# Scatter DMAs of routed rows placed between GpSimd's multiplications in the state-space scan

## The chip, the cores and the metric

One core of one Trainium2 chip runs the whole program. The metric is the device time of one execution in microseconds. Five engines take part: TensorE (PE in the rows), VectorE (DVE), ScalarE (ACT), GpSimd (POOL) and SyncE (SP), each with its own instruction queue; they meet only through semaphores and DMA completions.

## What is computed

A decoder layer on 32 sequences of 128 tokens with 128 channels: a selective state-space scan (16 states per channel, 256 inner channels), then attention against a context (16 heads of 8), then a mixture of 8 experts of which each token takes two; each of the three is added to its input and normed. Cut to what matters:

```python
xr = x @ W_in;  xs, res = split(xr);  u = silu(causal_conv(xs))
delta = softplus(...);  Bm, Cm = ...                    # from u @ W_x
hs = scan(exp(delta * A), delta * Bm * u)               # 16 states n
y  = einsum('bldn,bln->bld', hs, Cm) + u * D
x  = layernorm(x + (y * silu(res)) @ W_out)
x  = layernorm(x + attention(x, ctx))
x  = layernorm(x + sum_e wte[:, e] * ((silu(x @ w1[e].T) * (x @ w3[e].T)) @ w2[e].T))   # top 2 of 8 experts
```

## The kernel before

The tokens are cut into G = 8 groups of S = 4 sequences, T = 512 tokens each. A loop over m = 0..7 is written out on every engine, in an order set by hand; what follows a wait on an engine stands behind it. Each turn has two parts.

**Scan of group m**: states n = 0..15. For each state GpSimd forms `delta*u*B` (`times_b`, L420, into a ring of three buffers, so the product for state n + 3 waits for state n's scan), ScalarE forms the decay (`decay`, L588), VectorE runs two `tensor_tensor_scan` (`states`, L861) and, but for four states, multiplies by C (`times_c`, L868). States 2, 6, 9 and 12 (`POOLED`) are multiplied by C on GpSimd instead (`times_c`, L427, into one buffer `hc_pool`). TensorE adds each product into `y_ps` (`y_add`, L1339), broadcasts the B and C rows (L1315, L1326), and in between does convolutions and projections for groups m + 1 and m + 2. On TensorE the order around the last pooled product is fixed: row C 14, `y_add` of state 12, `y_add` of 13, residual, row C 15, `y_add` of 14, `y_last` (L1344). On GpSimd it is: `times_b` for 12 (at n = 9, behind `times_c` 9), 13, 14, 15 (at n = 10, 11, 12), then `times_c` for 12.

**Stage after the scan** (called the tail below, until attention's first exponentials): TensorE's output projection `first_out` (L1379), `values` (L1368), 12 matmuls that only keep it busy (L1387), transposes (L1396), queries (L1402), scores (L1424); VectorE's statistics (L899), norm (L914) and rotary products; ScalarE's exponentials (L623). GpSimd meanwhile makes the masks (`masks`, L440 and L443), scatters rows, adds a bias (`add_bo`, L454, which waits for VectorE's norm) and forms the next group's step sizes (L404, L406).

**The scatter**: once the top-2 experts of a group are known, each row of x2 goes to two places of the table `xg` in HBM. For group w that is eight indirect DMAs (4 sequences x 2 experts, 128 rows of 520 bytes each), L461, all on GpSimd's queue. Their places `pos` are written by VectorE at state n = 1 of scan w + 2 (`spots_out`). The experts' stage, which reads `xg`, begins after the last group. The scatters of groups 6 and 7 stand behind the loop.

SyncE issues loads in order: context and mask of the next group (the mask's after `masks`), then x three groups on, after `first_out`.

Of the kernel before, what the change touches and what calls it, by code (L numbers as in the profile page):

```python
# [14 lines left out]
S = 4  # L15
# [24 lines left out]
def build(nc, a, out):  # L40
    ctx = ExitStack()
    with ctx:
        def sb(name, shape, dt=F32):
            return ctx.enter_context(nc.sbuf_tensor(name, shape, dt))

        def sem(name):
            return ctx.enter_context(nc.semaphore(name))
# [99 lines left out]
        x2_all = sb("x2_all", [P, B, ROW])  # L147
# [10 lines left out]
        pos = sb("pos", [P, S, 2], I32)  # L158
# [51 lines left out]
        xg = nc.dram_tensor("xg", (E * STRIDE + P, ROW), F32, kind="Internal").ap()  # L210
# [13 lines left out]
        s = {n: sem(n) for n in names}  # L224
# [39 lines left out]
        def pooled_done(m, n):  # L264

            return len(POOLED) * m + POOLED.index(n) + 1
# [8 lines left out]
        def at(eng, name, count):  # L275
            if count > 0:
                eng.wait_ge(s[name], count)

        def parts(m):

            return (m - 1 if m else None), (m + 1 if m + 1 < G else None), (m + 2 if m + 2 < G else None)
# [84 lines left out]
        def _(pool):  # L366
# [34 lines left out]
            def step_size(m):  # L401
                at(pool, "softp", m + 1)
                at(pool, "a_ps", 2 * NST * m)
                g_.tensor_tensor(delta[:, :, :], zpos[:, :, :], zabs[:, :, :], ALU.add).then_inc(s["delta_sb"], 1)  # L404
                at(pool, "delta_sb", m + 1)
                g_.tensor_tensor(du[:, :, :], delta[:, :, :], u[:, m % 2], ALU.mult).then_inc(s["du_sb"], 1)  # L406
                at(pool, "du_sb", m + 1)
                for h in range(2):
                    last = g_.memset(delta[:, h, :].rearrange("p (s t) -> p s t", s=S)[:, :, 0:1], RESET)
                last.then_inc(s["delta_set"], 1)  # L410

            def times_b(m, n):
                at(pool, "du_sb", m + 1)
                at(pool, "b_sb", NST * m + n + 1)
                if n < 3:
                    at(pool, "s_ps", 16 * m)
                    at(pool, "h_sb", 2 * NST * m)
                else:
                    at(pool, "h_sb", 2 * (NST * m + n - 3) + 2)
                g_.tensor_tensor(bu[:, n % 3], du[:, :, :], b_row[:, n % 3, :].unsqueeze(1).broadcast_to((P, 2, T)), ALU.mult).then_inc(s["bu_sb"], 1)  # L420

            def times_c(m, n):
                at(pool, "h_sb", 2 * (NST * m + n) + 2)
                at(pool, "c_row_sb", pooled_done(m, n))
                before = POOLED.index(n) - 1
                at(pool, "y_sum", 17 * m + (POOLED[before] + 1 if before >= 0 else 0))
                g_.tensor_tensor(hc_pool[:, :, :], hst[:, n % 3], c_row[:, :].unsqueeze(1).broadcast_to((P, 2, T)), ALU.mult).then_inc(s["hc_pool_sb"], 1)  # L427

            def b_low(m, n):
                at(pool, "bc_mid_s", m + 1)  # L430
                if m:
                    at(pool, "hc_pool_sb", pooled_done(m - 1, 6))
                at(pool, "bu_sb", NST * (m - 1) + n)
                at(pool, "scat", (m - 3) * 2 * S * 16)
                g_.tensor_tensor(bc3[64:96, m % 2, :], bc_rest[64:96, :], bc_mid[64:96, :], ALU.subtract).then_inc(s["bc3_low"], 1)
                at(pool, "bc3_low", m + 1)

            def masks(g):
                at(pool, "mask_load", 16 * g + 16)
                g_.tensor_scalar(pad[:, :], mask_b[:, :], 0.0, NEG, ALU.is_equal, ALU.mult).then_inc(s["pad_sb"], 1)  # L440
                at(pool, "pad_sb", g + 1)
                at(pool, "s_ps", 16 * g)
                g_.tensor_tensor(mbias[:, :, :], pad[:, :].rearrange("p (s t) -> p s t", s=S),  # L443
                                 causal[:, :].unsqueeze(1).broadcast_to((P, S, L)), ALU.add).then_inc(s["mask_sb"], 1)

            def add_k(g):
                at(pool, "rotk_sb", 2 * g + 2)
                at(pool, "k_heads_sb", 4 * g)
                g_.tensor_tensor(qk[:, 1, :], rotk[:, 0, :], rotk[:, 1, :], ALU.add).then_inc(s["k_sb"], 1)

            def add_bo(g):
                at(pool, "x1_sb", S * g + S)
                at(pool, "wo_ps", 2 * g)
                g_.tensor_tensor(x1b[:, :, :], x1[:, :, :], bo_b[:, :].unsqueeze(1).broadcast_to((P, S, D)), ALU.add).then_inc(s["x1b_sb"], 1)  # L454

            def scatter(w):
                at(pool, "pos_sb", w + 1)
                at(pool, "row_sb", w + 1)
                for t in range(S):
                    for k in range(2):  # L460
                        pool.indirect_dma_start(xg[:, :], bass.IndirectOffsetOnAxis(ap=pos[:, t, k:k + 1], axis=0),  # L461
                                                x2_all[:, w * S + t, :], None).then_inc(s["scat"], 16)

            b_low(0, 0)
            for n in range(3):
# [1 line left out]
            for m in range(G):  # L467
                w, e, c = parts(m)
                for n in range(NST):
                    if n in POOLED and n != 12:  # L470
                        times_c(m, n)
                    if n + 3 < NST:
                        times_b(m, n + 3)
                    if n == 12:
                        times_c(m, n)
                    if n == 6 and e is not None:
                        b_low(e, 10)
                if m == 0:
                    at(pool, "w_later", 16 * NL)
                    add_k(0)  # L480
                masks(m)
                if m >= 2:
                    scatter(m - 2)
                add_bo(m)
                if e is not None:
                    at(pool, "q_sb", 2 * m + 1)
                    step_size(e)
                    add_k(e)
                    for n in range(3):
                        times_b(e, n)  # L490
            scatter(G - 2)
            scatter(G - 1)

            with pool.Fori(0, NT // 8) as it:
# [1209 lines left out]
```

## Time and profile before

| | |
|---|---|
| median of 3 runs | 1159.5 us (1154.22 to 1162.19) |
| the profiled execution | 1163.2 us |
| its span, first to last instruction | 1161.4 us |
| PE busy | 1022.0 us (88%) |
| DVE busy | 804.3 us (69%) |
| ACT busy | 759.5 us (65%) |
| POOL busy | 600.3 us (52%), with 64 scatter DMAs in 62.5 us |
| mean granted TensorE clock | 0.962 |

Busy shares are means over stages with different limits: GpSimd's 52% is made of stretches in which it has no gap and of long waits. The groups' turns take about 98 to 106 us each, from about 50 us to about 880 us of the span; then come the experts, and the last norm.

### The profile page before, as it was taken

What the parts mean: (1) busy time and instruction counts of PE and PEld (TensorE: products, weight loads), DVE (VectorE), ACT (ScalarE), POOL (GpSimd) and SP (SyncE); (2) the same over time, 40 slices, a digit from 0 to 9 for tenths busy, and PEclk for the clock granted to TensorE, in tenths of its full rate; (3) what the DMA queues carried; (4) which work ended last, traced back from release to release, by engine and by line L of the source; (5) the groups of instructions that cost most, each with busy time, mean ns of one, the idle gap of its engine ahead of it and who ended that gap; (6) DMA issues with size and microseconds to landing.
All of it is one profiled execution on the core that took longest, in us unless ns stands there. A gap on an engine that the chain in (4) does not pass through costs nothing.

```text
span 1161.4 us, 19208 instructions
## 1 busy us (share of the span) xinstructions
PE 1022.0 (88%) x5287; PEld 562.4 (48%) x5288; DVE 804.3 (69%) x1625; ACT 759.5 (65%) x2101; POOL 600.3 (52%) x388
## 2 busy tenths in 40 slices
PE   6799889989988988988899887977945999999987
PEld 2344544544454454445445534532533666666662
DVE  1597798788679868867986796798653544444437
ACT  2778877967786777679676775964742444444446
POOL 2595277278627936872794487379132333322210
PEclk9899999999899999999998999998987999999999
DMA  4000000000100000010000000000422111111134
GB/s 113 6 5 24 6 1 10 19 1 1 39 9 1 18 29 2 0 37 11 1 16 22 1 1 29 1 1 9 154 101 56 42 41 41 41 43 44 41 100 145
DMA packets 39402, 36.56 MB, mean 31 GB/s; under 512 B 6561, under 2 KB 35361, under 8 KB 38945
## 3 DMA queue, kind: packets, MB, share of 16 engines
q1 hardware_dynamic: 33792, 25.99, 7.7%
q0 software_dynamic: 4352, 8.99, 2.2%
q10 hardware_dynamic: 1184, 0.70, 0.3%
q8 instruction: 34, 0.56, 0.2%
q14 instruction: 40, 0.32, 0.1%
HBM read 23.99 MB, written 11.67 MB: 31 GB/s over the span
## 4 chain that ended last, share of the span: by engine, by line
PE 62%; ACT 14%; DVE 10%; issue 7%; POOL 4%; DMA 2%; SPq 1%; another core or an unknown queue 0%; DVEq 0%; POOLq 0%; ACTq 0%
PE y_ps L1339 13%; ACT prob L623 8%; PE bank L1616 6%; PE bank L1630 6%; PE bank L1617 6%; PE bank L1261 5%; DVE scan L861 4%; PE bank L1424 3%; PE y_ps L1622 3%; POOL hc_pool L427 2%; PE bank L1433 2%; PE bank L1457 2%; PE bank L1315 2%; PE bank L1326 1%; PE bank L1360 1%
## 5 line engine op out<-in xcount | busy, mean ns | idle before, releaser
L420 POOL TENSOR_TENSOR scan<-du,w 128x1024 f32<-128x1024 f32 x128 | 298.8, 2358 | 153.0 <-PE y_ps L1424 88.1
L861 DVE TENSOR_TENSOR_SCAN scan<-bank,scan 128x512 f32<-128x512 f32 x240 | 282.1, 1209 | 22.1 <-ACT bank L588 20.6
L588 ACT ACTIVATE bank<-delta,a_neg 128x512 f32<-128x512 f32 x240 | 163.5, 691 | 54.0 <-DVE scan L861 52.6
L1339 PE MATMUL y_ps<-w,ident 128*128 128x512 f32 x352 | 166.9, 596 | 0.0
L498 POOL DMA_INDIRECT y<-aoT,dest x72 | 69.2, 962 | 172.9 <-DVE aoT L1193 166.2
L868 DVE TENSOR_TENSOR w<-scan,bank 128x1024 f32<-128x1024 f32 x88 | 106.1, 1206 | 16.4 <-DVE scan L861 6.8
L571 ACT ACTIVATE w<-bank 128x512 f32<-128x512 f32 x121 | 71.3, 589 | 69.1 <-PE bank L1315 67.1
L1152 DVE TENSOR_TENSOR zpos<-zabs,bank 128x512 f32<-128x512 f32 x74 | 50.8, 687 | 78.8 <-PE bank L1617 77.7
L1339 PEld LDWEIGHTS y_ps<-w,ident 128*128 128x128 f32 x352 | 68.0, 193 | 62.0 <-issue 57.3
L623 ACT ACTIVATE prob<-y_ps,nmax 128x128 f32<-128x128 f32 x256 | 91.2, 430 | 0.4 <-DVE nmax L930 0.4
L623 ACT ACTIVATE prob<-bank,nmax 128x128 f32<-128x128 f32 x256 | 89.8, 387 | 2.2 <-DVE nmax L930 2.2
L461 POOL DMA_INDIRECT xg<-x_all,pos x64 | 62.5, 976 | 54.7 <-DVE pos L1022 36.7
L427 POOL TENSOR_TENSOR hc_pool<-scan,c_row 128x1024 f32<-128x1024 f32 x32 | 76.5, 2390 | 26.5 <-DVE scan L861 22.7
L1616 PE MATMUL bank<-w,qk 128*128 x148 | 76.8, 601 | 0.5 <-ACT qk L771 0.5
L1617 PE MATMUL bank<-w,qk 128*128 x148 | 76.1, 596 | 0.0
L1630 PE MATMUL bank<-prob,delta 128*128 x576 | 76.1, 275 | 0.0
L788 ACT ACTIVATE delta<-y_ps 128x512 f32<-128x512 f32 x72 | 43.0, 597 | 50.3 <-PE y_ps L1622 49.6
L1433 PE MATMUL bank<-ident,prob 128*128 128x128 f32 x512 | 69.4, 278 | 5.5 <-ACT pT L631 5.2
L775 ACT ACTIVATE zabs<-bank 128x512 f32<-128x512 f32 x74 | 44.2, 597 | 44.5 <-PE bank L1616 44.5
L1339 PE MATMUL y_ps<-hc_pool,ident 128*128 128x512 f32 x128 | 64.2, 626 | 8.9 <-POOL hc_pool L427 8.8
L1433 PEld LDWEIGHTS bank<-ident,prob 128*128 128x128 f32 x512 | 55.4, 141 | 33.4 <-issue 20.4
L1630 PEld LDWEIGHTS bank<-prob,delta 128*128 128x128 f32 x576 | 70.0, 192 | 0.0
(257 smaller groups left out, 2057.4 us busy)
## 6 DMA issues: line engine op xcount, KB each, us to landing
qk<-xg SPq DMA_DIRECT2D x79, 65.0 KB, 1.9
cn<-in_ctx SPq DMA_DIRECT2D x8, 256.0 KB, 2.9
mask_b<-in_mask SPq DMA_DIRECT2D x8, 256.0 KB
w<-in_w1T SPq DMA_DIRECT2D x1, 2048.0 KB, 8.8
w<-in_w3T SPq DMA_DIRECT2D x1, 2048.0 KB, 7.7
prob<-in_w2T SPq DMA_DIRECT2D x1, 2048.0 KB
u<-y SPq DMA_DIRECT2D x4, 512.0 KB, 5.9
w<-in_x SPq DMA_DIRECT2D x6, 256.0 KB, 3.0
```

What stands on the lines that cost most here:

```text
L420: g_.tensor_tensor(bu[:, n % 3], du[:, :, :], b_row[:, n % 3, :].unsqueeze(1).broadcast_to((P, 2, T)), ALU.mult).then_inc(s["bu_sb"], 1)
L427: g_.tensor_tensor(hc_pool[:, :, :], hst[:, n % 3], c_row[:, :].unsqueeze(1).broadcast_to((P, 2, T)), ALU.mult).then_inc(s["hc_pool_sb"], 1)
L571: A(b_row[:, n % 3, :], bank[1 if n < 3 else 0], ACT.Copy).then_inc(s["b_sb"], 1)
L588: A(bank[(6 if n else 4) + h], delta[:, h, :], ACT.Exp, scale=a_neg[:, h, n:n + 1]).then_inc(s["a_ps"], 1)
L623: last = A(prob[:, t % 2, c, j, :], bank[2 + c][:, j * L:(j + 1) * L], ACT.Exp, bias=nmax[:, t % 2, h:h + 1], accum_out=den[:, t % 2, h:h ...
L861: v_.tensor_tensor_scan(hst[:, n % 3, h, :], bank[(6 if n else 4) + h], bu[:, n % 3, h, :], 0.0, ALU.mult, ALU.add).then_inc(s["h_sb"], 1)
L868: TT(hc[:, i % 3], hst[:, n % 3], bank[2].unsqueeze(1).broadcast_to((P, 2, T)), ALU.mult).then_inc(s["hc_sb"], 1)
L1339: last = MM(y_ps[:, h], ident[:, :], hc_pool[:, h, :] if n in POOLED else hc[:, ON_DVE.index(n) % 3, h, :], start=False, stop=False, skip_ ...
L1433: last = TR(bank[6 + c % 2][:, j * L:(j + 1) * L], prob[:, t % 2, c, j, :], ident[:, :])
L1616: MM(bank[b], xsT[:, b, :], w1[:, bass.ds(e, 1), :].rearrange("p a f -> p (a f)"), start=True, stop=True).then_inc(s["up_ps"], 1)
L1617: MM(bank[2 + b], xsT[:, b, :], w3[:, bass.ds(e, 1), :].rearrange("p a f -> p (a f)"), start=True, stop=True).then_inc(s["up_ps"], 1)
L1630: last = MM(bank[6][:, b * P:(b + 1) * P], gT[:, b, c, :], w2[:, bass.ds(e, 1), c, :].rearrange("p a d -> p (a d)"), start=(c == 0), stop= ...
```

## The change

In scans m = 2 to 7 the eight DMAs of `scatter(m - 2)` no longer stand together behind `masks(m)`. One of them is issued at the end of each of GpSimd's steps n = 7 to 14 of scan m; each call has its waits on `pos_sb` and `row_sb`, both counts being reached since state 1. The scatters of groups 6 and 7 stay as they were. No instruction of work is added or removed.

```diff
-            def scatter(w):
+            def scatter(w, which=range(2 * S)):
                 at(pool, "pos_sb", w + 1)
                 at(pool, "row_sb", w + 1)
-                for t in range(S):
-                    for k in range(2):
-                        pool.indirect_dma_start(xg[:, :], bass.IndirectOffsetOnAxis(ap=pos[:, t, k:k + 1], axis=0),
-                                                x2_all[:, w * S + t, :], None).then_inc(s["scat"], 16)
+                for i in which:
+                    t, k = divmod(i, 2)
+                    pool.indirect_dma_start(xg[:, :], bass.IndirectOffsetOnAxis(ap=pos[:, t, k:k + 1], axis=0),
+                                            x2_all[:, w * S + t, :], None).then_inc(s["scat"], 16)
...
                     if n == 6 and e is not None:
                         b_low(e, 10)
+                    if m >= 2 and 7 <= n < 7 + 2 * S:
+                        scatter(m - 2, (n - 7,))
                 if m == 0:
                     at(pool, "w_later", 16 * NL)
                     add_k(0)
                 masks(m)
-                if m >= 2:
-                    scatter(m - 2)
                 add_bo(m)
```

## Rows read from the trace of the kernel before

**Rows 1.** The page: chain that ended last by engine; the scatter's group.

```profile
PE 62%; ACT 14%; DVE 10%; issue 7%; POOL 4%; DMA 2%; SPq 1%; another core or an unknown queue 0%; DVEq 0%; POOLq 0%; ACTq 0%
L461 POOL DMA_INDIRECT xg<-x_all,pos x64 | 62.5, 976 | 54.7 <-DVE pos L1022 36.7
```

**Rows 2.** Timeline, POOL, m = 3: start us, us, what, [idle before <-releaser].

```profile
378.05 4.67 POOL L420 TENSOR_TENSOR scan<-du,w 128x1024 f32<-128x1024 f32 x2
...
385.00 9.40 POOL L420 TENSOR_TENSOR scan<-du,w 128x1024 f32<-128x1024 f32 x4
394.92 2.38 POOL L427 TENSOR_TENSOR hc_pool<-scan,c_row 128x1024 f32<-128x1024 f32 x1 [0.53 <-issue]
...
399.40 1.29 POOL L443 TENSOR_TENSOR mbias<-pad,causal 128x512 bf16<-128x512 f32 x1
400.85 1.06 POOL L461 DMA_INDIRECT xg<-x_all,pos  x1 [0.15 <-issue]
402.21 0.96 POOL L461 DMA_INDIRECT xg<-x_all,pos  x1 [0.30 <-issue]
...
412.29 1.26 POOL L454 TENSOR_TENSOR x1b<-x,bo_b 128x512 f32<-128x512 f32 x1 [1.55 <-DVE x L914]
```

**Rows 3.** Timelines, DVE and PE, m = 3, states 11 to 14.

```profile
386.71 2.33 DVE L861 TENSOR_TENSOR_SCAN scan<-bank,scan 128x512 f32<-128x512 f32 x2
...
397.36 1.98 PE L1339 MATMUL y_ps<-hc_pool,ident 128*128 128x512 f32 x4 [0.23 <-POOL hc_pool L427]
...
399.39 1.88 PE L1339 MATMUL y_ps<-w,ident 128*128 128x512 f32 x4
```

**Rows 4.** Timelines, POOL and PE, m = 6 and m = 7, around state 12.

```profile
703.81 2.37 POOL L427 TENSOR_TENSOR hc_pool<-scan,c_row 128x1024 f32<-128x1024 f32 x1
...
706.24 3.14 PE L1339 MATMUL y_ps<-hc_pool,ident 128*128 128x512 f32 x4 [3.49 <-POOL hc_pool L427]
...
709.60 2.25 PE L1339 MATMUL y_ps<-w,ident 128*128 128x512 f32 x4
...
803.67 3.78 PE L1339 MATMUL y_ps<-hc_pool,ident 128*128 128x512 f32 x4 [3.80 <-POOL hc_pool L427]
...
807.67 2.71 PE L1339 MATMUL y_ps<-w,ident 128*128 128x512 f32 x4
```

**Rows 5.** Timeline, POOL: the product of state 12 in m = 1, 2, 4, 5.

```profile
190.37 2.38 POOL L427 TENSOR_TENSOR hc_pool<-scan,c_row 128x1024 f32<-128x1024 f32 x1 [0.53 <-issue]
...
288.80 2.38 POOL L427 TENSOR_TENSOR hc_pool<-scan,c_row 128x1024 f32<-128x1024 f32 x1 [0.53 <-issue]
...
497.19 2.38 POOL L427 TENSOR_TENSOR hc_pool<-scan,c_row 128x1024 f32<-128x1024 f32 x1 [0.53 <-issue]
...
599.43 2.39 POOL L427 TENSOR_TENSOR hc_pool<-scan,c_row 128x1024 f32<-128x1024 f32 x1 [0.52 <-issue]
```

**Rows 6.** Timeline, ACT: attention's first exponential in m = 1, 2, 3, 5, 6.

```profile
210.05 0.36 ACT L623 ACTIVATE prob<-bank,nmax 128x128 f32<-128x128 f32 x1
...
312.76 0.36 ACT L623 ACTIVATE prob<-bank,nmax 128x128 f32<-128x128 f32 x1
...
418.44 0.36 ACT L623 ACTIVATE prob<-bank,nmax 128x128 f32<-128x128 f32 x1
...
623.44 0.36 ACT L623 ACTIVATE prob<-bank,nmax 128x128 f32<-128x128 f32 x1
...
726.79 0.36 ACT L623 ACTIVATE prob<-bank,nmax 128x128 f32<-128x128 f32 x1
```

**Rows 7.** Windows, m = 1 and m = 2 tails: stretch, its us, busy, then PE clock, DMA.

```profile
192.80:210.10 17.30, 16.71 (x78) 10.24 (x80) 13.22 (x38) 14.80 (x26) 6.48 (x4) 1.00 0.11 32
291.20:313.40 22.20, 19.59 (x78) 10.95 (x80) 13.70 (x38) 15.72 (x29) 16.66 (x13) 0.87 0.15 48
```

**Rows 8.** Timeline, DVE: second statistics pair in the tails of m = 1, 3, 7.

```profile
203.32 0.46 DVE L899 BATCH_NORM_STATS2 stats<-bank 128x6 f32<-128x128 f32 x2
...
410.10 0.50 DVE L899 BATCH_NORM_STATS2 stats<-bank 128x6 f32<-128x128 f32 x2 [1.36 <-remote]
...
817.44 0.49 DVE L899 BATCH_NORM_STATS2 stats<-bank 128x6 f32<-128x128 f32 x2
```

## The prediction

> **What bounds the kernel now.** I read the page's chain first [rows 1]: PE has 62% of it, POOL only 4%, so a little GpSimd time must sit at one place of each scan. The timelines show where. In m = 3 POOL runs with no gap from 378.05 to 394.40: products for states 10 and 11, the product by C for state 9, then four products (12 to 15) [rows 2]. Half a microsecond later comes the product of state 12, and PE starts its sum 0.05 us after that one ends (394.92 + 2.38 = 397.30, then 397.36) [rows 2, 3]. What follows on PE up to the tail is PE work in fixed order, so a delay of this product is a delay of the group. The slack ahead of it is 0.53 us, the same in m = 1 to 5 [rows 2, 5]; in m = 6 and 7, where PE has fewer projections to do, it is none, and PE already idles 3.49 and 3.80 us for it [rows 4].
>
> The scatter, eight DMAs at a pitch of 1.26 us (0.96 busy and 0.30 gap), stands in the tail, where POOL has room: the bias add behind it still waits 1.55 us for VectorE's norm [rows 2]. So by GpSimd's own queue it costs nothing today. But the tail itself is longer with it. From the end of state 12's product to the first exponential: m = 1, without a scatter, 210.05 - 192.75 = 17.3 us; m = 2, 312.76 - 291.18 = 21.6; m = 3, 418.44 - 397.30 = 21.1; m = 5, 623.44 - 601.82 = 21.6 [rows 2, 5, 6]. The windows show PE with the same 78 matmuls in both tails but a clock of 0.87 against 1.00 [rows 7], and the DVE rows show one place: the second statistics pair follows at once in m = 1, and in m = 3 waits 1.36 us for a signal the profile cannot place [rows 8]. I can name the coincidence with scatters in flight, not its cause.
>
> **The change, part by part.** Nothing is added; 48 DMAs (8 in each of m = 2 to 7) move.
>
> *Where they land.* Behind n = 7 to 11 come five DMAs, all ahead of state 12's product (which is issued at n = 12 behind the product for 15). Those at n = 12, 13, 14 come after it and before the masks.
>
> *Price of one.* No row shows an indirect DMA between two tensor operations. From below: gap 0.15 and the first one's 1.06 us, 1.21 [rows 2]. From above: the same plus the 0.30 that follows each DMA, and some growth, say 1.65. The nearest row is the pitch of 1.26; a DMA behind a tensor operation took 0.10 more than one behind a DMA (1.06 against 0.96), so I take 1.35 us. The waits on `pos_sb` and `row_sb` are long met; they are in the 0.15 gap.
>
> *Five in the packed stretch.* 5 x 1.35 = 6.75 us. In m = 2 to 5 the slack of 0.53 comes off: 6.2 us each. In m = 6 and 7 nothing comes off: 6.75 each. VectorE feels it earlier but less: product 12 would end at 387.35 + 2.7 = 390.05, and its scan began at 386.71 + 1.17 = 387.88 [rows 2, 3], so VectorE slips about 2.2 us, inside the 6.2. GpSimd's ring is no extra wait: product 15 needs scan 12, which is done by about 393.5, and starts at 398.6 or later.
>
> *The clock.* In m = 6 and 7 PE's clock was at the lower level when it came out of its wait for this product: the sum after 3.49 us of idle took 3.14 us where 1.98 is usual, the next 2.25 against 1.88; after 3.80 us, 3.78 and 2.71 [rows 3, 4]. That is 1.5 and 2.6 us lost at 1.2 GHz. In m = 2 to 5 the new idle would be 4 to 6 us, so I add the mean, 2.1 us each. In m = 6 and 7 that toll is paid already.
>
> Loss: 4 x (6.2 + 2.1) + 2 x 6.75 = 33.2 + 13.5 = 46.7 us.
>
> *The three behind it and the tail.* They end about 4 us after state 12's product, the masks 3.3 us later; scores want the mask some 17 us after that product. Hidden, with 9 us to spare; that cover gone they would cost 7 us. SyncE's mask load goes behind `masks` by about 4 us relative to the group, and is not wanted until the next scan's end. The projection, statistics and `values` then run with no scatter in flight, as in m = 1. What that returns is read from the turns, product to product: m = 1 to 2 took 288.80 - 190.37 = 98.4 us; m = 2 to 3, 106.1; m = 3 to 4, 102.3; m = 4 to 5, 102.2 [rows 2, 5]. So tails of m = 2, 3, 4 return 7.7, 3.8 and 3.8 us (the 7.7 holds a longer stretch at the low clock behind the tail). m = 5 has m = 2's tail (21.6), so 7.7. In m = 6 the tail is 726.79 - 706.18 = 20.6 [rows 4, 6], of which 1.5 is the clock toll: 1.8 returned. In m = 7 the statistics do not wait [rows 8]: nothing. Gain: 24.8 us.
>
> Sum: 46.7 - 24.8 = 22 us slower. The profiled execution took 1163.2 us (span 1161.4), 3.7 above the median of 1159.5; against it the sum is 1185, against the median 1181.5.
>
> **The rivals.**
>
> *The tail is not relieved.* If its length is not the scatter's doing (groups 0 and 1 differ in nothing else that I see, but it is coincidence so far), or if three DMAs suffice to keep the signals late, nothing is returned: 1159.5 + 46.7 = 1206. For it: I have no cause. Against: m = 7, whose scatter ends as its projection does, shows no such wait.
>
> *Small or no loss.* The DMA at its lower bound and no fall of the clock in m = 2 to 5: 4 x 5.5 + 2 x 6.05 = 34 lost, 24.8 returned: +9, 1169, within 1%. For it: idle split in two pieces may not lower the clock. Against: shorter waits than those I expect were followed by it in m = 6 and 7.
>
> *Faster: descriptors are written beside the multiplication.* If the DMA's 0.96 us of POOL did not hold the next tensor operation, the scan would lose nothing and the tail gain would stand alone: 1159.5 - 24.8 = 1134.7. It decides below 0.9 us for one DMA without the clock toll (30 DMAs, less 4 x 0.53, equal 24.8), or 0.6 with it. For it: no row has an operation directly behind a scatter that was not waiting for something else. Against: the DMAs themselves never overlap, and each is booked on the engine. The Trainium skill (GPSIMD Engine Reference, "When to use GPSIMD") says that only a pair of GpSimd's eight cores generates the descriptors, and its "Instruction dispatch" that a core goes on to the next instruction once its own share is done. By that rule six cores run ahead, but a multiplication is complete only when all eight are, so it would still end late by the pair's time; no run here shows it.
>
> **How the numbers follow.** The forecast 0.68; tail not relieved 0.13; small loss 0.13; overlap 0.06. The likeliest's own range: price 1.21 to 1.65 and toll 1.5 to 2.6 give losses of 40 to 58, so +15 to +33, 1174 to 1193. For 8 in 10 the range takes in most of the two neighbours: 1168 to 1206. About 1% (11.6 us) is what a measurement can tell from none: slower 0.82, same 0.12, faster 0.06.
>
> **What would show it.** Right: in m = 2 to 5, state 12's product starts with DMAs in the stretch ahead of it, PE's sum behind it idles 4 to 6 us and runs long; in m = 6 and 7 that idle is about 10 us; a DMA costs POOL 1.2 to 1.65 us between products; the second statistics pair no longer waits for a remote signal; from product to first exponential 17 to 20 us; the bias add waits longer for VectorE. Wrong: PE's wait there unchanged (overlap), tails of 21 us or more (not relieved), or new waits of PE, VectorE or ScalarE between n = 7 and n = 14 that no row of POOL explains.

## The result, and the profile after

The changed kernel took 1177.18 us (median; 1176.89 to 1177.59), the kernel before beside it 1156.95 (1154.22 to 1162.19): a ratio of 1.017 with an interval of 1.0127 to 1.0212. It is slower by 20 us, inside the range, 4 us under the forecast of 1181.5. On which chip this pair ran is not on record. The profiled execution of after has a span of 1175.5 us.

The page of after: shares of the chain by engine, then two groups, PE's sums of the products by C that GpSimd makes, and the scatter (busy us, mean ns | idle before, releaser). The last row is from the page of before, for the group that [rows 1] doesn't hold.

```profile
PE 57%; ACT 15%; DVE 11%; issue 8%; POOL 7%; DMA 2%; SPq 0%; POOLq 0%; DVEq 0%; ACTq 0%
L1339 PE MATMUL y_ps<-hc_pool,ident 128*128 128x512 f32 x128 | 75.2, 718 | 39.7 <-POOL hc_pool L427 39.5
L461 POOL DMA_INDIRECT xg<-x_all,pos x64 | 64.3, 1004 | 50.4 <-DVE pos L1022 36.5
```

```profile
L1339 PE MATMUL y_ps<-hc_pool,ident 128*128 128x512 f32 x128 | 64.2, 626 | 8.9 <-POOL hc_pool L427 8.8
```

PE now waits 39.5 us for GpSimd's products by C where it waited 8.8, and the matmuls behind those waits take 11 us more in all (75.2 against 64.2). POOL's share of the chain went from 4% to 7%.

The timeline of POOL in after, m = 3 (start us, us, what, [idle before <-releaser]); before's are [rows 2].

```profile
375.87 2.36 POOL L420 TENSOR_TENSOR scan<-du,w 128x1024 f32<-128x1024 f32 x1
378.39 1.06 POOL L461 DMA_INDIRECT xg<-x_all,pos  x1 [0.16 <-issue]
...
388.93 2.37 POOL L420 TENSOR_TENSOR scan<-du,w 128x1024 f32<-128x1024 f32 x1
391.47 1.01 POOL L461 DMA_INDIRECT xg<-x_all,pos  x1 [0.17 <-DVE scan L861]
392.51 2.36 POOL L420 TENSOR_TENSOR scan<-du,w 128x1024 f32<-128x1024 f32 x1
395.03 1.01 POOL L461 DMA_INDIRECT xg<-x_all,pos  x1 [0.17 <-issue]
396.08 2.35 POOL L420 TENSOR_TENSOR scan<-du,w 128x1024 f32<-128x1024 f32 x1
398.38 2.34 POOL L427 TENSOR_TENSOR hc_pool<-scan,c_row 128x1024 f32<-128x1024 f32 x1
...
415.48 1.28 POOL L454 TENSOR_TENSOR x1b<-x,bo_b 128x512 f32<-128x512 f32 x1 [7.67 <-DVE x L914]
```

With a DMA between them, two products start 392.51 - 388.93 = 3.58 us apart, and 396.08 - 392.51 = 3.57. Without one they are 2.35 apart (9.40 / 4 in [rows 2]). So one DMA costs 1.22 us of GpSimd: 1.01 for itself, 0.17 ahead of it and 0.04 more. The state-12 product at 398.38 follows with no idle; before, it was preceded by 0.53 us of it.

PE behind that product in after, m = 3, then its two waits for GpSimd in m = 6; before's are [rows 3, 4].

```profile
400.78 3.64 PE L1339 MATMUL y_ps<-hc_pool,ident 128*128 128x512 f32 x4 [5.31 <-POOL hc_pool L427]
...
404.48 1.88 PE L1339 MATMUL y_ps<-w,ident 128*128 128x512 f32 x4
...
701.58 3.43 PE L1339 MATMUL y_ps<-hc_pool,ident 128*128 128x512 f32 x4 [2.51 <-POOL hc_pool L427]
...
716.88 3.78 PE L1339 MATMUL y_ps<-hc_pool,ident 128*128 128x512 f32 x4 [5.76 <-POOL hc_pool L427]
```

The tail in after, m = 3, on VectorE: the two pairs of statistics ([rows 8] for before).

```profile
412.25 0.50 DVE L899 BATCH_NORM_STATS2 stats<-bank 128x6 f32<-128x128 f32 x2 [1.08 <-PE bank L1379]
...
412.95 0.46 DVE L899 BATCH_NORM_STATS2 stats<-bank 128x6 f32<-128x128 f32 x2
```

The wait of 1.36 us for a remote signal is gone: the second pair starts 0.70 us behind the first. Where the time went, turn by turn, worked out from the timelines of POOL and ACT. "Delay" is the growth from the exponential that opens attention's last quarter to the next state-12 product (before's lengths 58.4, 59.3, 58.4, 58.4, 57.6, 54.1); "tail" is from the end of that product to the first exponential; "attention" is from there to its last quarter.

```
m                   2      3      4      5      6      7     sum
delay            +5.7   +4.7   +5.7   +5.6   +5.3   +6.3   +33.3
tail before     21.58  21.14  21.12  21.62  20.60  20.40
tail after      18.82  18.95  18.99  19.03  19.61  19.38   -11.7
attention        -2.5      0      0   -2.5      0      0    -4.9
```

That is +16.7; the start is 1.7 shorter and the end 0.8, and the spans differ by 14.1 (1175.5 against 1161.4). The medians differ by 20, since before's profiled execution (1163.2) was 6 over its own median.

Much of what the tail gives back is PE's clock. In before's tail of m = 3 PE waits 1.74 and 0.91 us (0.47 in m = 1), which is 2.2 of the 3.85 us by which that tail is longer than in m = 1. Behind these waits its matmuls run at the lower clock, and that is most of the rest. In m = 2 this stretch goes on into attention, where it is the 2.5 us of the last row. Windows of before: the tail's end in m = 1, then in m = 2, the start of attention in m = 2, the tail's end in m = 3 (granted clock of PE: third number from the end):

```profile
203.00:210.10 7.10, 6.52 (x41) 4.22 (x41) 5.38 (x28) 4.92 (x13) 3.29 (x2) 1.00 0.13 38
306.70:312.80 6.10, 6.09 (x16) 2.27 (x16) 2.90 (x13) 2.56 (x6) 3.73 (x2) 0.57 0.00 0
312.80:318.00 5.20, 5.20 (x15) 2.83 (x15) 2.67 (x7) 5.00 (x30) 1.09 (x3) 0.52 0.01 2
412.80:418.40 5.60, 5.50 (x18) 2.57 (x20) 2.61 (x13) 2.58 (x6) 3.53 (x3) 0.70 0.00 0
```

### The profile page after: what moved, and what is told of

Read it like the earlier page. It is cut to its first block, busy times and chain, and to the rows that moved or that the text cites. A ratio compares the mean times of both kernels' runs of the same rounds, so it can differ in the third digit from the quotient of the medians.

```text
span 1175.5 us, 19250 instructions
## 1 busy us (share of the span) xinstructions
PE 1015.8 (86%) x5287; PEld 559.0 (48%) x5288; DVE 807.0 (69%) x1625; ACT 758.8 (65%) x2101; POOL 602.9 (51%) x388
## 4 chain that ended last, share of the span: by engine, by line
PE 57%; ACT 15%; DVE 11%; issue 8%; POOL 7%; DMA 2%; SPq 0%; POOLq 0%; DVEq 0%; ACTq 0%
PE y_ps L1339 14%; ACT prob L623 8%; PE bank L1616 6%; PE bank L1630 5%; PE bank L1617 5%; DVE scan L861 4%; PE bank L1261 4%; POOL hc_pool L427 3%; PE bank L1424 3%; PE y_ps L1622 3%; PE bank L1433 2%; POOL xg L461 2%; POOL scan L420 2%; PE bank L1457 2%; PE bank L1315 1%
## 5 line engine op out<-in xcount | busy, mean ns | idle before, releaser
L861 DVE TENSOR_TENSOR_SCAN scan<-bank,scan 128x512 f32<-128x512 f32 x240 | 284.8, 1212 | 50.5 <-POOL scan L420 18.8
L1339 PE MATMUL y_ps<-w,ident 128*128 128x512 f32 x352 | 167.1, 597 | 0.0
L571 ACT ACTIVATE w<-bank 128x512 f32<-128x512 f32 x121 | 71.2, 589 | 60.2 <-PE bank L1315 58.4
L1339 PE MATMUL y_ps<-hc_pool,ident 128*128 128x512 f32 x128 | 75.2, 718 | 39.7 <-POOL hc_pool L427 39.5
L1339 PEld LDWEIGHTS y_ps<-w,ident 128*128 128x128 f32 x352 | 68.1, 193 | 63.8 <-issue 58.8
L1433 PEld LDWEIGHTS bank<-ident,prob 128*128 128x128 f32 x512 | 55.4, 141 | 33.4 <-issue 20.4
L623 ACT ACTIVATION_READ_ACCUMULATOR prob<-y_ps,nmax 128x1 f32 x256 | 70.5, 277 | 0.0
```

What stands on the lines that cost most here:

```text
L623: last = A(prob[:, t % 2, c, j, :], bank[2 + c][:, j * L:(j + 1) * L], ACT.Exp, bias=nmax[:, t % 2, h:h + 1], accum_out=den[:, t % 2, h:h ...
L861: v_.tensor_tensor_scan(hst[:, n % 3, h, :], bank[(6 if n else 4) + h], bu[:, n % 3, h, :], 0.0, ALU.mult, ALU.add).then_inc(s["h_sb"], 1)
L1339: last = MM(y_ps[:, h], ident[:, :], hc_pool[:, h, :] if n in POOLED else hc[:, ON_DVE.index(n) % 3, h, :], start=False, stop=False, skip_ ...
L1433: last = TR(bank[6 + c % 2][:, j * L:(j + 1) * L], prob[:, t % 2, c, j, :], ident[:, :])
```

## The experiments

The theory of the prediction has two halves. *Loss:* GpSimd's time ahead of state 12's product delays PE, and PE's wait is followed by the lower clock. *Gain:* a scatter in flight in the tail makes PE's signals late there, and taking it away returns that. The rivals: the loss is the DMAs' traffic, not GpSimd's time; the tail's length has another cause, such as the program's place in memory or PE's instruction fetches. Experiments were run in three groups, each with its own runs of before. Lines shift by up to four where an edit adds some (L1341 and L1343 there are L1339 here).

**The scatter later, and the same kernels shifted.** Four kernels, on one chip. The first puts all eight DMAs behind the bias add:

```diff
                 masks(m)
+                add_bo(m)
                 if m >= 2:
                     scatter(m - 2)
-                add_bo(m)
```

> The eight DMAs of the scatter stand together behind the bias add (L454) instead of between the masks and it, so they start some 4 us after TensorE's output projection. Both sides of the change are separated: the packed stretch ahead of state 12's product stays free (slip 0), and the projection runs with no scatter in flight. Theory A (the tail is long only where scatters are in flight while TensorE fetches its next 16 KB of instructions, which falls on the projection): tails of 17.3 us in m = 2 to 5, turns of 98.4 us, 1132 to 1140 us. Theory B (scatters slow the engines wherever they are): the 4 us come back in the first scores instead, turns of 102 us, within 1% of the kernel before.

The second puts them behind the keys (in m = 7 behind the bias add):

```diff
                 masks(m)
-                if m >= 2:
-                    scatter(m - 2)
                 add_bo(m)
                 if e is not None:
                     at(pool, "q_sb", 2 * m + 1)
                     step_size(e)
                     add_k(e)
+                if m >= 2:
+                    scatter(m - 2)
+                if e is not None:
                     for n in range(3):
```

> The eight DMAs stand together behind the addition of the keys (L449), where GpSimd waits 12.6 us for the scores anyway (in m = 7 behind the bias add). Theory A: as with the scatter behind the bias add, 1132 to 1140 us, if no fetch of TensorE falls into these ten microseconds; there is one some 11 us ahead of the end of attention, and if it is hit the turn gets 2 to 4 us back. Theory B: within 1% of the kernel before.

The last two add spare matmuls at PE's start, which shift its instruction stream: once in before, once in after.

```diff
+            keep_warm(32)
             x_t(0, 3)
             pe.wait_ge(s["w_load"], 16 * NW)
```

> The kernel before, with 32 more matmuls on TensorE ahead of its first transposes, where it waits for weights. They move every later instruction of TensorE by half a 16 KB block, so its fetch leaves the output projection and falls on about states 10 to 12 of the scan, ahead of the scatter. Nothing else changes. Theory A: the tails of m = 2 to 5 fall from 21.4 to 17.3 us, 1132 to 1142 us. Theory B: tails as before, time as before to 0.3%.

> The changed kernel with the same 32 matmuls ahead, so that TensorE's fetch falls on states 10 to 12, between the spread scatters. Theory A: signals of TensorE come late there, the scan's second half grows by 1 to 4 us a turn: 1182 to 1200 us. Theory B: as the changed kernel, 1177 us to 0.3%.

On this chip the kernel before took 1135.73 us (1133.9 to 1138.46, 14 runs), 21 us less than beside after. Against it: behind the bias add 1142.31, ratio 1.0058 (1.0036 to 1.008); behind the keys 1135.44, 0.9996 (0.9985 to 1.0006); before shifted 1131.6, 0.9953 (0.9936 to 0.997); after shifted 1174.7, 1.0336 (1.0318 to 1.0353).

All four had the tails of m = 2 to 5 short: 17.28 to 17.30 us, and 18.94 to 19.08 for after shifted. That holds for before shifted too, whose scatter runs at its old place in the tail. Its timelines in m = 3: POOL's first and last DMA and the bias add; VectorE's statistics.

```profile
390.39 1.06 POOL L461 DMA_INDIRECT xg<-x_all,pos  x1 [0.17 <-issue]
...
399.32 0.96 POOL L461 DMA_INDIRECT xg<-x_all,pos  x1 [0.30 <-issue]
400.30 1.28 POOL L454 TENSOR_TENSOR x1b<-x,bo_b 128x512 f32<-128x512 f32 x1
...
396.71 0.50 DVE L899 BATCH_NORM_STATS2 stats<-bank 128x6 f32<-128x128 f32 x2 [1.08 <-PE bank L1379]
...
397.40 0.46 DVE L899 BATCH_NORM_STATS2 stats<-bank 128x6 f32<-128x128 f32 x2
```

The scatter was at its sixth of eight DMAs when the statistics came, and no signal was late. So a scatter in the tail alone does not lengthen it: the prediction's gain needs a second condition. Without it nothing is returned, and the change costs its whole loss: from m = 1 to m = 7, state 12's products of after shifted lie 629.6 us apart (188.54 to 818.13), those of before shifted 587.7 (187.62 to 775.28), so +41.9 us; end to end 1174.7 against 1131.6, +43. The second condition could be the shift (instruction fetches fall elsewhere) or the chip, and these four don't tell which: before itself has no trace from this chip, only its time. The expectation that a fetch among the spread DMAs would make signals late (1182 us or more for after shifted) failed. Behind the bias add the tail is clean, but the time is over the 1132 to 1140 expected, since attention in m = 3 to 6 lasts 1.4 to 4.2 us longer: the step size and the keys stand behind eight DMAs (the product of the step size at 411.64, against 402.18 in before shifted).

**The pair again, and the dose.** On a second chip, where before took 1160.12 (1153.11 to 1169.37, 19 runs). First before itself and after itself, to see whether the pair repeats:

> The kernel before, word for word, for its profile beside the other runs of this study, in which it takes 1135.7 us and not the 1157 us of the prediction's comparison. If the long tails (21.1 to 21.6 us in m = 2 to 5) were what the 21 us between them are, this profile has tails of 17.3 us in m = 2 to 5, turns of 98.4 us and the same waits at the product of state 12 as rows 2 to 4. If the chip is simply faster, every stretch is shorter by 1.8%.

> The changed kernel, word for word. If the late signals in the tail were the only thing that differs between the two comparisons, the changed kernel, whose tails were clean already, takes the same here as there, 1175 to 1178 us, and the change costs 41 us instead of 20: 4 x (6.1 - 0.53 + 1.6) + 2 x 6.1, with 1.22 us for one DMA and 1.6 us for the clock as its first profile shows. If this chip is faster as a whole, it takes 1155 us.

Before again: 1157.63, ratio 0.9998 (0.9961 to 1.0035). After again: 1180.02, 1.019 (1.0154 to 1.0225). So before has its long tails on this chip too, not the clean ones that before again was to test for, and the change costs 20 us and not 41. After's stretches repeat in m = 2 to 5 (PE's wait in m = 3 5.32 us, tails 18.8 to 19.0); in m = 6 PE's wait at state 12 is 7.18 us, where it was 5.76. Before's tails are 21.1, 21.1, 21.1 and 21.5 in m = 2 to 5, and only m = 5 has the longer attention (22.97 us). So its turn from m = 2 to 3 is 102.25 us here, and was 106.1 in the execution that the prediction read.

Then two DMAs in the packed stretch and six behind state 12's product:

```diff
+                    if m >= 2 and n in (7, 8):
+                        scatter(m - 2, (n - 7,))
+                    if m >= 2 and n == 12:
+                        scatter(m - 2, range(2, 2 * S))
...
-                if m >= 2:
-                    scatter(m - 2)
```

> Two of the eight DMAs (behind n = 7 and 8) instead of five ahead of state 12's product; the other six stand behind that product, before the masks. The slip should be 2 x 1.22 - 0.53 = 1.9 us in m = 2 to 5 and 2.4 us in m = 6 and 7, 12.5 us in all, with no toll on the clock since TensorE waits only 2 us in m = 2 to 5: 1148 us. If every DMA in the scan costs what TensorE loses in clock too, 1154 us. If a scatter's cost were its traffic and not its place in GpSimd's order, two of eight moved cost as much as eight: 1170 us or more.

1154.03, ratio 0.9948 (0.9922 to 0.9973). In m = 3 GpSimd's idle ahead of state 12's product is gone, and PE waits for its sum:

```profile
391.62 2.37 POOL L427 TENSOR_TENSOR hc_pool<-scan,c_row 128x1024 f32<-128x1024 f32 x1
...
394.05 3.29 PE L1341 MATMUL y_ps<-hc_pool,ident 128*128 128x512 f32 x4 [1.59 <-POOL hc_pool L427]
```

Two cost 2 x 1.22 - 0.53 = 1.91 us by this case's numbers; the delay measured in m = 4 and 5 is 1.9. The price scales with the number ahead of the product. The clock is another matter: a wait of only 1.59 us was followed by a sum of 3.3 to 3.7 us in m = 2, 3 and 5, and by one of the usual 1.98 in m = 4. The tails say the same, 19.0, 19.0 and 18.8 us against 17.29 in m = 4. So in these turns the toll does not grow with the wait; it is there or not. The time is 15 us above that of the next experiment, which has no DMA in the packed stretch; the 12.5 of slip expected and 4.9 of toll in the tails cover that. The expectation's figure without the toll, 1148, and the one for traffic, 1170 or more, both failed.

And three where GpSimd has time, five behind the product (the scan's last B rows wait for the scatter, so that wait was raised by the three that are issued ahead of it):

```diff
-                at(pool, "scat", (m - 3) * 2 * S * 16)
+                at(pool, "scat", (m - 3) * 2 * S * 16 + (48 if m >= 3 else 0))
...
+                    if m >= 2 and n in (0, 4, 5):
+                        scatter(m - 2, ((0, 4, 5).index(n),))
+                    if m >= 2 and n == 12:
+                        scatter(m - 2, range(3, 2 * S))
```

> Also spread over the scan, but where GpSimd waits anyway: one DMA behind each of n = 0, 4 and 5, five behind state 12's product, none between n = 6 and it (and a wait for the three to land ahead of the write at n = 6). If the loss is the packed stretch's alone, this takes what the kernel before takes, 1134 to 1138 us. If a scatter DMA inside the scan costs in itself (descriptor writes beside VectorE's scans, traffic), three of them cost 3/5 of the 41 us or some share of it: 1150 us or more.

(The edit also takes out the call behind `masks`, as above.) 1138.93 (1138.3 to 1140.93), ratio 0.9834 (0.9801 to 0.9868): 1.7% faster than before, and 3.5% faster than after (1180.02), on this chip. Its timelines in m = 3, POOL, PE and DVE:

```profile
343.37 2.35 POOL L420 TENSOR_TENSOR scan<-du,w 128x1024 f32<-128x1024 f32 x1 [6.39 <-ACT w L573]
345.88 1.06 POOL L461 DMA_INDIRECT xg<-x_all,pos  x1 [0.16 <-issue]
...
362.36 1.01 POOL L461 DMA_INDIRECT xg<-x_all,pos  x1 [0.17 <-issue]
364.61 2.36 POOL L427 TENSOR_TENSOR hc_pool<-scan,c_row 128x1024 f32<-128x1024 f32 x1 [1.24 <-DVE scan L863]
...
387.63 2.38 POOL L427 TENSOR_TENSOR hc_pool<-scan,c_row 128x1024 f32<-128x1024 f32 x1 [0.52 <-issue]
...
390.07 1.98 PE L1341 MATMUL y_ps<-hc_pool,ident 128*128 128x512 f32 x4 [0.23 <-POOL hc_pool L427]
...
399.88 0.49 DVE L901 BATCH_NORM_STATS2 stats<-bank 128x6 f32<-128x128 f32 x2 [1.08 <-PE bank L1381]
...
400.58 0.46 DVE L901 BATCH_NORM_STATS2 stats<-bank 128x6 f32<-128x128 f32 x2
```

Behind the two DMAs after states 4 and 5 GpSimd still waits 1.24 us for VectorE, state 12's product keeps its 0.52 of slack, PE's sum takes 1.98 us, and the last five DMAs end at 396.23, ahead of the projection. Tails are 17.29 us in m = 2 to 5: gain without loss.

**Shift or chip; and GpSimd's time alone.** Again on the second chip, where before took 1160.48 (1156.58 to 1167.58). The shifted before and the scatter behind the keys, unchanged:

> The kernel before with 32 matmuls ahead of TensorE's first transposes, once more, now beside an execution of the kernel before that has the long tails, if there is one (its time says so: 1157 us, against 1136 without them). Theory A (long tails need TensorE's instruction fetch and a scatter in flight together): tails of 17.3 us and 1132 to 1138 us wherever it runs. Theory B (scatter traffic lengthens the tail by itself where conditions are those of the slow comparison): as the kernel before, 1157 us.

> The eight DMAs together behind the addition of the keys, once more. Where the kernel before takes 1157 us: 1136 us if its tail is clean and nothing comes back in attention (theory A with no fetch hit), 1145 us or more if the lateness follows the scatter to its new place. Where the kernel before takes 1136 us: the same as it, as the first time.

Before shifted: 1154.93 (1149.21 to 1157.2), 0.9936 (0.9909 to 0.9962), with long tails, 21.0 to 21.1 us in m = 2 to 5. Its VectorE in m = 3:

```profile
400.27 0.50 DVE L899 BATCH_NORM_STATS2 stats<-bank 128x6 f32<-128x128 f32 x2 [1.08 <-PE bank L1379]
...
402.45 0.50 DVE L899 BATCH_NORM_STATS2 stats<-bank 128x6 f32<-128x128 f32 x2 [1.40 <-remote]
```

The same instructions as in the shifted before above, which had none of it. The fetches were my suspect. In before, a packet of queue q8 falls within the scatter in each of m = 2 to 5 (at 301, 407, 510 and 611 us). I take q8 for PE's instructions, since 32 spare matmuls on PE move its packets. In before shifted none falls within a scatter in m = 2 to 5 (the nearest in m = 3 is at 378 us), and the signal is late all the same. The DMA view of m = 3's scatter, first before again (395 to 406 us), then before shifted (394 to 404 us):

```profile
q0 software_dynamic: 224, 0.47, 13.5%
q1 hardware_dynamic: 394, 0.39, 10.7%
q8 instruction: 1, 0.02, 0.8%
q14 instruction: 1, 0.01, 0.5%
```

```profile
q0 software_dynamic: 224, 0.47, 14.7%
q1 hardware_dynamic: 212, 0.22, 8.3%
q14 instruction: 1, 0.01, 0.3%
```

So PE's fetch is not needed, and the shift is not the condition: the same kernel has the wait on one chip and not on the other. The first chip was used in one session only, so chip and session are not told apart.

The scatter behind the keys took 1188.85 (1187.88 to 1192.78), ratio 1.0245 (1.0194 to 1.0297), where it had equalled before on the first chip. Its tails are 17.29 us, but attention up to its last quarter takes 27.9 to 30.9 us instead of 20.4. PE in m = 2's attention there, and below it the same place on the first chip:

```profile
320.07 1.13 PE L1425 MATMUL y_ps<-scan,qk 32*128 32x512 f32 x4
325.12 1.08 PE L1434 MATMUL bank<-ident,prob 128*128 128x128 f32 x4 [3.93 <-issue]
```

```profile
321.04 1.13 PE L1425 MATMUL y_ps<-scan,qk 32*128 32x512 f32 x4
322.10 1.09 PE L1434 MATMUL bank<-ident,prob 128*128 128x128 f32 x8
```

In both, the eight DMAs run beside it (315.8 to 325.9 and 316.8 to 326.8). In the slower one the waits of that stretch are for signals that no record places, and GpSimd's next product waits 11.0 us for attention's scores (2.4 us on the first chip):

```profile
POOL scan L420 <- PE y_ps L1425: 11.0, 1, 11.0
PEld bank L1434 <- issue: 6.7, 5, 4.7
ACT pT L632 <- remote: 5.5, 1, 5.5
```

On this chip the lateness follows the scatter from the tail into attention. Whether it takes PE's short matmuls, or anything else that these two stages have and the scan has not, was not tested.

Last, all eight DMAs directly behind state 12's product (the call behind `masks` is out again), then the same with five small additions on GpSimd in place of the five DMAs of the packed stretch (the additions compute nothing that is used):

```diff
+                    if m >= 2 and n == 12:
+                        scatter(m - 2)
```

> All eight DMAs together directly behind state 12's product, ahead of the masks: the packed stretch is free, and against the kernel before the scatter only starts 3.3 us earlier, so it ends about when TensorE's fetch begins. Theory A: most of the lateness goes, tails of 17.3 to 19 us in m = 2 to 5, 1136 to 1145 us. Theory B (eight DMAs in the tail are eight DMAs in the tail): as the kernel before to 0.5%. In both, masks end 10 us after the product and scores want them 17 us after it: no new wait.

```diff
+                    if m >= 2 and 7 <= n < 12:
+                        at(pool, "filled", 5 * (m - 2) + n - 7)
+                        g_.tensor_tensor(filler[:, :, :], rope[:, :, 0:118], rope[:, :, 0:118], ALU.add).then_inc(s["filled"], 1)
+                    if m >= 2 and n == 12:
+                        scatter(m - 2)
```

> As the kernel with all eight DMAs behind state 12's product, but with five additions on GpSimd (128 x 472, about 1.2 us each, into a tile that nothing reads) where the change has its five DMAs ahead of that product, behind n = 7 to 11. It puts GpSimd's time into the packed stretch and leaves the DMAs' descriptors and traffic out of it. If the loss is GpSimd's time alone: the slip (5.6 us), TensorE's waits (5.3 us) and the toll (1.6 us) of the changed kernel, and its time, 1174 to 1183 us. If descriptors or traffic beside the scans carry part of it: nearer to the kernel with none, by that part.

Without additions: 1146.29 (1145.33 to 1154.32), ratio 0.989 (0.9828 to 0.9952). PE's wait ahead of the sum is 0.21 to 0.24 us in m = 2 to 5, so the DMAs cost nothing behind the product; the last one ends at 400.6 instead of 396.2, and the tails are 18.2 to 20.3 instead of 17.29, since PE's L1379 signals late (VectorE waits 2.71 us for it in m = 3, against 1.08). The time lies between the two forecasts: the lateness is smaller than in before, not gone.

With them: 1174.07 (1173.52 to 1177.26), ratio 1.0116 (1.0067 to 1.0165), 27.8 us above. POOL, PE, m = 3:

```profile
378.14 0.97 POOL L481 TENSOR_TENSOR filler<-rope 128x472 f32<-128x472 f32 x1
379.07 2.36 POOL L421 TENSOR_TENSOR scan<-du,w 128x1024 f32<-128x1024 f32 x1
...
396.67 2.38 POOL L428 TENSOR_TENSOR hc_pool<-scan,c_row 128x1024 f32<-128x1024 f32 x1
...
399.10 3.78 PE L1343 MATMUL y_ps<-hc_pool,ident 128*128 128x512 f32 x4 [4.18 <-POOL hc_pool L428]
```

An addition costs 379.07 - 378.14 = 0.93 us; five less the slack of 0.53 are 4.1, and PE waits 4.12 to 4.2. The sum behind it takes 3.78 us. No DMA stands in that stretch, so the loss needs none: it is GpSimd's time and PE's clock. The additions turned out shorter than the 1.2 us expected, so slip and wait are smaller than after's, and the comparison shows the kind of loss and not its exact size; the time is at the lower end of the 1174 to 1183 expected. (In m = 3 to 5 the turn grows by 4.9, 0.8 more than the wait. A stretch at the lower clock stands at the end of attention ahead of it: at 342.8 us, for instance, PE's L1461 takes 0.49 us where 0.28 to 0.30 is usual.)

## Why the prediction held, point by point

- **Where they land, and that the stretch is packed:** right. Five DMAs stand ahead of state 12's product, which follows without idle.
- **Price of one DMA:** 1.22 us, at the lower bound of 1.21; 1.35 was taken. The pitch of DMA to DMA (1.26) was the wrong neighbour: its gap of 0.30 is between two DMAs, and between products there is 0.17. Over 30 DMAs that is 3.9 us of overestimate. Delay expected 38.3 us (4 x 6.2 + 2 x 6.75), measured 33.3. This is the term that was most off.
- **PE's wait:** 4 to 6 us expected in m = 2 to 5, measured 5.31 to 5.32. In m = 6 and 7 about 10 was expected and 5.76 and 5.97 measured (7.18 and 5.99 in after again). This step was wrong in form, not in its sum: PE already waits 2.51 us at state 9's product in m = 6, where before it did not, and the turns were delayed by 5.3 and 6.3 of the 6.75. A delay of GpSimd shows at every point where PE meets it, not at the last alone.
- **VectorE's slip:** 2.2 us expected, inside PE's. VectorE's idle ahead of its scans (L861) that GpSimd's products end rose from 4.0 to 21.2 us over the kernel. It is no loss of its own as far as the turns show: they grew by what GpSimd's DMAs take. The slip of one scan was not measured.
- **The clock's toll:** 2.1 us each in m = 2 to 5 expected, from 1.5 and 2.6. Measured, the tail stands 1.5 to 1.7 above 17.29: 6.6 in all against 8.4. It lies in the sum, 3.5 to 3.7 us instead of 1.98; the matmuls after it are back at 1.88 in m = 3. The row with 1.5 of loss was the better one. The mean of two unlike rows was not.
- **The three behind the product, and the masks:** hidden, as forecast; the bias add waits 7.67 us (1.55 before).
- **The gain:** 24.8 expected; 23.2 worked out (11.7 in the tails and 4.9 in attention, with the toll of 6.6 that the tails now contain). It holds two things: PE's longer waits behind the late signals, and the lower clock that follows them, to which the windows put the 4.9. By turns 6.8, 3.8, 3.8, 6.8, 1.0, 1.0 against 7.7, 3.8, 3.8, 7.7, 1.8, 0. That 7.7 in m = 2 was this one execution's: before again has 3.8 there. It is part of why that execution was 6 us over its median, and so of why the profiled pair differs by 14 us and the medians by 20.
- **The sum:** 33.3 + 6.6 - 23.2 = 16.7 in the turns, expected 22. The loss was 6.8 too high (5.0 of delay, 1.8 of toll) and the gain 1.6, and the two errors offset in part. That the medians come out within 2 us of the sum is partly luck: the terms were read from one execution that was 6 us slow, and against that execution the forecast was 1185 and the profiled time 1177.3.
- **The rival that the tail is not relieved** (1206, that is + 46.7) failed here, but it is what happens on the first chip, where there is nothing to relieve: +43 us, 1174.7 against 1131.6. The prediction said that it could name the coincidence and not the cause. The loss was understood; the gain, half as large, was a coincidence read off the rows, and it held here because the pair ran where the signals are late. What makes them late is not found.
- **The small loss** (DMA at its lower bound and no toll) was half right: the price is at the bound, the toll is there. That split idle keeps the clock up did not hold in after's m = 6: behind waits of 2.51 and 5.76 us the sums took 3.43 and 3.78. In after again the first of these waits was followed by a sum of 1.98, so one wait does not always bring it.
- **The overlap rival** failed: 1.22 us per DMA, where below 0.6 or 0.9 was needed. In the trace the next product starts 0.03 to 0.04 us behind the DMA's end and takes its usual 2.36 us. The Trainium skill (GPSIMD Engine Reference, "When to use GPSIMD") says that it is a pair of GpSimd's cores that generates the descriptors. Whatever the other cores may do meanwhile shortens nothing in this trace.

## What to carry to other kernels

An operation that is moved out of a stretch where its engine has room, into one where the engine is packed ahead of a product that the bounding engine waits for, costs its time there, and the bounding engine can pay again in its clock. Look for the gaps of the issuing engine first: three DMAs behind states 0, 4 and 5, and five behind the last product, gave the whole gain at no delay, and eight directly behind the product gave two thirds of it. A gain that rests on a coincidence in the trace should be tried on more than one chip before it is counted.

## What the runs showed of the hardware that I had not expected

- The kernel before takes 1135.7 us on one chip and 1157 to 1160 in the other comparisons. The traces place the difference in signals of PE that arrive late while GpSimd's indirect DMAs are in flight beside PE's work in the tail or in attention. The semaphore events of before, where the time is the longer one, show this in m = 2 to 5: in each, the second of L1379's two signals comes 1.7 to 2.5 us after its matmul's modelled end, and L1368's 3.7 to 3.8. In m = 6 it is 2.2 and 2.1, in m = 7 0.7 and 0.7. In m = 0 and 1, which have no scatter, it is 0.01, and so it is in every scan of the four kernels profiled on the first chip and of after. The page shows such a wait as "remote" or "issue".
- It is larger in attention: with the scatter behind the keys, the latest of the signals of L1434, L1425 and L1458 came 6.0 to 7.5 us late in each of m = 2 to 6.
- Where signals of PE are late, some events of ScalarE's and VectorE's signals are missing in the trace, so it is not shown that PE's alone are late. On the first chip no engine has a signal over 0.3 us late.
- After's products and waits were the same on both chips (5.3 us, tails 18.8 to 19.1); only what the scatter meets differs.
- What remains open: why one chip (or session) does it and another not, and by what path a scatter delays a signal. PE's instruction fetch is excluded by the shifted kernel; the traffic of the descriptors, and the writes of the rows themselves, were not separated. Whether the early scatter is also faster on the first chip was not tried.
